# Gated cross-attention and mixture block: the preparation of the next batches laid out anew over the heads, its PSUM banks alternating by batch

## What is computed

```
q = layernorm(x) @ wq + bq ; k = ctx @ wk + bk ; v = ctx @ wv + bv      # 16 heads of width 16
logits = q k^T / sqrt(16) + (1 - mask) * -1e9
attn = softmax(logits) * group_prob
x = x + tanh(g_xattn) * (attn @ v @ wo + bo)
x = x + tanh(g_ffn) * (shared MLP + top-2 of 8 expert MLPs)(rmsnorm(layernorm(x)))
```

## Time and profile before

| | |
|---|---|
| median of 3 runs | 700.69 us |
| the profiled execution | 701.35 us, its span 699.1 us |
| PE busy | 601.9 us (86%) |
| DVE busy | 484.6 us (69%) |
| ACT busy | 394.0 us (56%) |
| POOL busy | 287.0 us (41%) |
| attention's 16 steps | from about 47 us to 344 us of the span |
| granted TensorE clock in the attention | 1.00, 2.4 GHz |
| HBM traffic | 55.43 MB read, 28.30 MB written |

### The profile page before, as it was taken

How to read it: one execution, slowest core, us unless ns; L and a number is a source line. 1 busy time by engine, 2 the same in 40 slices (tenths; PEclk the granted TensorE clock), 3 DMA queues, 4 the chain that set the end, 5 groups by cost and what they waited for, 6 DMA issues and landing times. The chain is left out here.

```text
span 699.1 us, 19138 instructions
## 1 busy us (share of the span) xinstructions
PE 601.9 (86%) x6150; PEld 500.8 (72%) x6150; DVE 484.6 (69%) x1304; ACT 394.0 (56%) x994; POOL 287.0 (41%) x327
## 2 busy tenths in 40 slices
PE   2689999999999999999757999989979989899950
PEld 2457777787777778777536888778868878688850
DVE  5858778877877877778695866565654746556537
ACT  4468888888888888887716423253533434324320
POOL 7303344443443334446530077405535534456120
PEclk9799999999999999999975999999999999899995
DMA  8525557775555655633050042213343332441218
GB/s 226 148 79 145 154 135 190 193 187 131 133 133 137 138 141 138 154 87 68 1 181 1 8 153 99 90 42 128 103 154 119 91 120 91 112 145 46 61 49 311
DMA packets 86600, 84.28 MB, mean 121 GB/s; under 512 B 17879, under 2 KB 80341, under 8 KB 86430
## 3 DMA queue, kind: packets, MB, share of 16 engines
q1 hardware_dynamic: 78686, 70.83, 37.5%
q0 software_dynamic: 2976, 8.16, 3.2%
q10 hardware_dynamic: 4896, 4.76, 2.7%
HBM read 55.43 MB, written 28.30 MB: 120 GB/s over the span
## 5 line engine op out<-in xcount | busy, mean ns | idle before, releaser
L928 PE MATMUL ps<-ident,probs 112*125 112x112 f32 x768 | 192.5, 277 | 2.5 <-POOL probs L509 1.4
L714 ACT ACTIVATE probs<-probs,negmax 112x375 f32<-112x375 f32 x256 | 154.9, 608 | 25.9 <-DVE negmax L1230 25.7
L1082 PE MATMUL ps<-w,arena 128*128 128x256 f16 x1152 | 142.1, 280 | 17.7 <-DVE arena L1373 17.3
L764 ACT ACTIVATE arena<-ps,b 128x256 f32<-128x256 f32 x192 | 79.4, 472 | 137.3 <-PE ps L1071 137.1
L928 PEld LDWEIGHTS ps<-ident,probs 112*125 112x125 f32 x768 | 138.8, 188 | 23.7 <-issue 9.0
L1230 DVE CUSTOM_DVE_ANT_0 probs<-ps,neg 112x375 f32<-112x375 f32 x256 | 137.2, 538 | 11.9 <-issue 9.5
L1082 PEld LDWEIGHTS ps<-w,arena 128*128 128x128 f16 x1152 | 111.4, 100 | 43.7 <-DVE arena L1373 29.0
L509 POOL TENSOR_TENSOR probs<-probs,gp_in 112x375 f32<-112x375 f32 x64 | 58.7, 917 | 181.4 <-ACT probs L714 181.4
L1237 DVE TENSOR_TENSOR arena<-ps,gpT 125x336 f32<-125x336 f32 x192 | 97.0, 506 | 46.4 <-PE ps L928 45.8
L1071 PE MATMUL ps<-probs,w 128*128 128x256 f16 x816 | 91.9, 273 | 0.1
L1071 PEld LDWEIGHTS ps<-probs,w 128*128 128x128 f16 x816 | 79.7, 98 | 9.6 <-issue 0.3
(11 more groups left out here) (173 smaller groups left out, 828.9 us busy)
## 6 DMA issues: line engine op xcount, KB each, us to landing
k_scratch<-kT SPq DMA_DIRECT2D x96, 93.8 KB
kst<-k_scratch SPq DMA_DIRECT2D x64, 140.6 KB, 3.6
w1s<-in_L_ffn_ew_dram SPq DMA_DIRECT2D x8, 1024.0 KB, 5.2
w2s<-in_L_ffn_ew_dram SPq DMA_DIRECT2D x8, 1024.0 KB, 5.6
x_sent<-y_sb SPq DMA_DIRECT2D x12, 516.0 KB, 5.5
ctx_in<-in_ctx_dram SPq DMA_DIRECT2D x16, 375.0 KB
probs<-x_sent ACTq DMA_DIRECT2D x18, 258.0 KB
arena<-y_back SPq DMA_DIRECT2D x7, 512.0 KB, 7.2
```

What stands on the lines that cost most here:

```text
L714: act.activation(probs[:, n % PROBS], probs[:, n % PROBS], ACT.Exp, bias=negmax[:, p, n:n + 1], scale=-1.0, accum_out=rowsum[:, p, ORDER[n ...
L764: act.activation(hid32[:, f], ps[:, f // 2 % 4, f % 2 * TILE:(f % 2 + 1) * TILE], ACT.Relu, bias=b1[:, f, e:e + 1]).then_inc(h_relu, 1)
L928: mm = pe.transpose(ps[0:KP, PT[n % 2], c * S:(c + 1) * S], probs[:, n % PROBS, c * KP:(c + 1) * KP], ident[0:S, 0:S])
L1082: mm = pe.matmul(ps[:, 4 + a, 0:D], hid[:, u, f, a * P:(a + 1) * P], w2[:, p, w, f], start=(f == 0 and j == 0), stop=(f == NF - 1 and j == 2))
```

## The change

The same matmuls are issued; their order, their readers and their banks differ.

- The slots move. Of the batch after next, the context is now at heads 10 and 11 (slots 12 and 13 of the old offset stood at heads 12 and 13) and the keys at heads 12 to 15 (before: head 15 and heads 0 to 2 of the next step). Of the next batch, the values are at heads 2 to 7 (before 5 to 10), chunk 2 first, and the group probability at head 8 (before 11). Heads 0, 1 and 9 have no slot (before 3, 4 and 14). `PREP` is gone.
- `prep_bank(p, piece)` alternates the two banks by piece and by the batch's parity.
- The group probability is taken out of PSUM by DVE (`take_group_probs`, new semaphore `gp_turned`) and no longer by ACT. ACT's pieces stand after its exponentials 0, 1, 5, 9 (keys, keys, values, values), 12 and 13 (context of the batch after next).
- `POOL_HEADS` is (1, 5, 9, 13), was (2, 6, 8, 12). POOL's side work is in another order: `make_neg` after its third head of the step, was after its first.
- DVE makes the keys' low halves at heads 0 and 1 (was 1 and 3), the inverse at 1 (was 0), the division at 13 (was 8).
- SP stores and stacks half 0, then half 1, and loads the mask between storing and stacking half 0. The two stores of high halves no longer wait for the low half.

```diff
-PREP = 4
-        POOL_HEADS = (2, 6, 8, 12)
+        POOL_HEADS = (1, 5, 9, 13)
+        def prep_bank(p, piece):
+            return PR[(p + piece) % 2]
...
                 for n, c in enumerate(K_PARTS):
+                    if c == LO:
+                        sp.wait_ge(in_x[0], 16)
+                        sp.wait_ge(prep_lo, low)
...
                 load_queries(t + 1, 1 - p)
-                for m in range(ND):
-                    store_keys(t + 1, m)
+                store_keys(t + 1, 0)
                 if more:
                     next_mask(t + 1, 1 - p)
-                for m in range(ND):
-                    stack_keys(t + 1, 1 - p, m)
+                stack_keys(t + 1, 1 - p, 0)
+                store_keys(t + 1, 1)
+                stack_keys(t + 1, 1 - p, 1)
...
                     times_group_prob(t, n, p, own if k == 0 else None)
+                    if k == 0 and more:
+                        context_high(t + 2, p, own + 1, turned, slice(0, KC))
                     if k == 0 and not first:
                         spread_inverse(t - 1)
-                    if k == 0 and not last:
+                    if k == 1 and more:
+                        context_low(t + 2, p)
+                    if k == 2 and not last:
                         done = pool.compute_val(H * t + SC_FREE)
                         pool.wait_ge(consts, 4)
                         pool.wait_ge(sc_read, done)
                         make_neg(t + 1, 1 - p, ahead)
-                    if k == 1 and more:
-                        context_high(t + 2, p, own + 1, turned, slice(0, KC))
-                    if k == 2 and more:
-                        context_low(t + 2, p)
...
-            pieces = {0: 1, 3: 2, 5: 3, 11: 4, 13: 5, 14: 6}
+            pieces, context_pieces = {0: 2, 1: 3, 5: 4, 9: 5}, {12: 0, 13: 1}
...
-                    if t_after and n == H - 1:
-                        prep_piece(t + 2, 0, p)
+                    if t_after and n in context_pieces:
+                        prep_piece(t + 2, context_pieces[n], p)
...
+            def take_group_probs(b, p):
+                dve.wait_ge(prep_mm, 7 * b + 7)
+                dve.tensor_copy(gpT[:, p], bank(prep_bank(p, 6), KP, KC * S).rearrange("p (c q) -> p c q", c=KC)).then_inc(gp_turned, 1)
...
-                    if prep and n in (1, 3):
-                        keys_low(t + 1, n // 3)
-                    if n == 0 and not first:
+                    if prep and n in (0, 1):
+                        keys_low(t + 1, n, 1 - p)
+                    if prep and n == 9:
+                        take_group_probs(t + 1, 1 - p)
+                    if n == 1 and not first:
                         invert_sums(t - 1, 1 - p)
-                    if n == 8 and not first:
+                    if n == 13 and not first:
                         divide(t - 1, 1 - p)
```

More of the change, by code:

```diff
@@ L832, in queries, with turn_ctx @@
                     mm.then_inc(q_mm, 1)
-            def turn_ctx(b, k, third):
+            def turn_ctx(b, k, p, third):
                 if third == 0:
@@ L856, in keys @@
                 w, a = PASSES[third]
-                mm = pe.matmul(bank(PR[m], P, S2), wpair[:, 1, w, part, m * P:(m + 1) * P], ctxT[:, a, part, 0:S2],
+                mm = pe.matmul(bank(prep_bank(p, 2 + m), P, S2), wpair[:, 1, w, part, m * P:(m + 1) * P], ctxT[:, a, part, 0:S2],
                                start=(part == 0 and third == 0), stop=(part == 1 and third == 2))
@@ L952, in _ @@
             turn_x(Q_TILES[0])
-            for n in range(2):
+            for n in range(CTX_SLOT, K_SLOT):
                 prep_whole(0, n, 0, 1)
             queries(0)
-            for n in range(2, 7):
+            for n in range(K_SLOT, H):
                 prep_whole(0, n, 0, 1)
             turn_x(Q_TILES[1])
-            for n in range(7, H - 1):
+            for n in range(V_SLOT, GP_SLOT):
                 prep_whole(0, n, 0, 1)
@@ L982, in prep_third @@
                 def prep_third(n, third):
-                    if n + PREP < H and t_next:
-                        prep_slot(t + 1, n + PREP, 1 - p, loads, third)
-                    if n + PREP >= H and t_after:
-                        prep_slot(t + 2, n + PREP - H, p, None, third)
+                    if n < CTX_SLOT:
+                        if t_next:
+                            prep_slot(t + 1, n, 1 - p, loads, third)
+                    elif t_after:
+                        prep_slot(t + 2, n, p, None, third)
                 for n in range(H):
                     turn_probs(t, n, 0)
-                    if first and n == 0:
-                        for m in range(2, PREP):
-                            prep_whole(t + 1, m, 1 - p, loads)
                     prep_third(n, 0)
@@ L1002, in step @@
                     prep_third(n, 2)
+                    if first and n < ND:
+                        for m in range(2):
+                            prep_whole(t + 1, K_SLOT + 2 * n + m, 1 - p, None)
                     if n % QUAD == 1:
@@ L1211, in _ @@
                 queries_low(c)
+            take_group_probs(0, 0)
             dve.wait_ge(small_out, 4)
@@ L1233, in weigh @@
             def weigh(t, n, p):
+                if n == 0:
+                    dve.wait_ge(gp_turned, t + 1)
                 dve.wait_ge(pt_made, 16 * t + n + 1 + PROBS_FREE)
```

78 lines of the change are left out of this document (40 added, 38 removed).

## The result

The change made the kernel slower by 2.75%: the median of five runs is 718.39 us (715.88 to 728.05), that of the kernel before beside it 698.46 us (696.97 to 701.76), the ratio 1.0275 with a 95% interval of 1.0246 to 1.0304. The prediction said 699.6 us, no measurable change, in a range of 688 to 709. It missed in both.

The account below looks back on a forecast made before the run. PE was taken to set the step, so only its idle time could be won. Removed waits (-20.5 us) and new ones (+12.6, +6.8) summed to -1.1 us, from 700.69 to 699.6 us, range 688 to 709.

Parts of the forecast that it names:

- The two waits that go: PE's waits at the value slot (15 x 0.65 us) and second context slot (14 x 0.77) vanish: 20.5 us, bounds 16.3 and 21.4.
- The prediction's first part: What bounds the kernel: PE sets the step, only its idle time can be won, about 1.2 us a step.
- POOL at heads 5 and 13: PE waits for POOL's late products: 0.72 to 0.86 us at head 13, about 0.45 at head 5 (6.8 us in all).
- The stacked keys at head 12, in the loop: PE's score waits 0.8 us for keys stacked behind the mask; with head 13, 0.9 us together, 12.6 us in all.
- the two prices weighed there: Landing of SP's second key stacking: 3.5 or 4.2 us by the trace's rows, 2.3 by the Trainium skill's rule.
- The sum: Whole kernel: -20.5 us for removed waits, +12.6 for heads 12 and 13, +6.8 for head 5, giving -1.1 us.
- The third rival: Second key stacking lands late, PE's score at head 12 waits 1.8 us in 13 steps: 711 us, or 705; chance 0.17.

Follow-up runs that it names:

- The best version: Changed kernel with both stores first, mask last, batch 1's keys before step 0, POOL heads 0, 4, 8, 12, DVE's inverse at head 0, division at 11: ratio 0.9805.
- the variant without a wait for stacked keys: Changed kernel with SP's order as both key stores, both stackings, then the mask's load: ratio 1.0075 against the kernel before.

## Why the prediction was wrong

**The two waits that go: right, but 0.25 us a step too dear.** Both went. I priced them nearer to the weight loads, 0.65 + 0.77 = 1.42 us, and took the matmuls' side (16.3 us for all) for the lower bound. The matmuls' side was the price. In the kernel before a step of 18.80 us has 17.63 of busy PE, so its idle time is 1.17 us. The best version removes nearly all of it and gains 1.1 us a step. The prediction's first part had said "about 1.2 us a step by its matmuls", and its sum then took off more idle time than there was. The term is 16 us and not 20.5.

**POOL at heads 5 and 13: right, head 5 somewhat dear.** Forecast 0.72 to 0.86 us at head 13 and 0.45 at head 5. In the variant without a wait for stacked keys PE idles 0.65 or 0.75 us at head 13 and 0.23 or 0.37 at head 5, by turns. A step with the longer two:

```profile
228.66 0.36 PE L938 MATMUL ps<-ident,probs 112*125 112x112 f32 x1 [0.37 <-POOL probs L514]
...
238.23 0.36 PE L938 MATMUL ps<-ident,probs 112*125 112x112 f32 x1 [0.75 <-POOL probs L514]
```

In the changed kernel itself the wait at head 12 covers that of head 13, as said, and head 5 shows the same 0.23 or 0.37, 0.30 in the mean.

**The stacked keys at head 12, in the loop: right mechanism, somewhat small.** Forecast 0.8, by the landings of the earlier trace rows 1.1 or 1.8; it was 1.17. With 0.30 at head 5 that is 1.47 us of new idle time a step for 1.17 of old, and steps of 19.1 for 18.8. Of the two prices weighed there, that of the rows was the better one: the two stackings of 86.08 took 3.0 and 3.5 us to land, those of half 0 in the loop (229.4) 3.1 and 3.4. The 2.3 us that I had worked out from the Trainium skill ("DMA: Bandwidth & Descriptors") was too short, as the prediction had supposed; the page fits it to DMAs that GpSimd issues, and these are SyncE's. The experiment with `make_neg` at the first head shows the cause to be the one named: the wait goes, and the step is 18.7.

**The first steps: the step that failed, 13.3 us.** The sum had nothing for them. (Of the 13.3 us, 1.5 are the 0.3 us a step of the term above.) The third rival named the mechanism ("the two halves are now stored one after the other, with a landing waited out for each", and the query stores) and then turned it down with the sentence "after them SP still has about 2.5 us to spare in a step". None of the prediction's rows shows that figure, but it was fair for the old order: between the last load and the next store of keys SP stood still for 1.7 to 4.2 us in a round (85.6 to 89.83 in the one above). It was never set against what the new order adds to a round. That is 5.6 us from the first store to the end of the stacking (13.8 against 8.2), more than there was: each half's landing is waited out with nothing to issue but the mask, where before it ran under the other half's stores. A round of 18.8 us less 1.7 to 4.2 and with 5.6 more is 20.2 to 22.7 us, and 20.1 to 22.1 was measured. The rival's price was wrong too. I gave it 0.8 to 1.8 us in each of 13 steps; it was 0.5 to 1.3 us in ten of them and a stall of 3.2 to 3.4 us in three, by turns with the short ones. I read this as a queue that falls behind and is given its time back by PE's long wait. SP's own idle time ahead of the mask fits: 2.0, 1.6 and 1.7 us in the rounds that end in a long wait of PE, 4.0, 4.3 and 6.5 us in those behind them. No run tests that reading. By the orders tried, this part is removed by issuing both stores first, in the changed kernel, and brought in by the new order alone, in the kernel before.

**The clock.** PE's clock was not in the prediction. The table before it gives 1.00 for the whole attention, and that is so from step 1 on, but step 0 had 0.93 already in the kernel before. Of the 5.3 us of the longest step 2.7 are matmuls at half clock. No variant kept a long stall and the clock both, so the split rests on busy times.

**Step 0: not costed, 6.7 us.** The sum counted heads 0 and 1 only for DVE's low keys, in the later steps. In step 0 the keys of batch 1 are made on the spot, in the same two heads as their reader and a POOL head. Moved ahead of the step, they give back 6.0 of it, half of that by the clock. What is left of the difference, 1.1 us, comes with more work: PE has 237 matmuls up to the first inverse there, and 202 in the kernel before, and the last three steps are shorter for it.

**What the range missed.** Its upper end of 709 lay between the third rival's two prices, 705 and 711 us, for a wait of at most 1.8 us in every step. The two terms left out came to 20.0 us at the last inverse, nearly all of the 21.5 that was lost. The other 5.5 us of the two profiled spans lie behind the attention and are not a loss that I can show: the median of the runs is only 19.9 us later.

**Open.** What lets the clock fall in one step and not in another is not shown: a stall of 1.66 us in the kernel before with the new order was followed by the lower clock, one of 1.64 us in the changed kernel with the mask's rows earlier was not. Why the kernel before lost most of its low-key wait with POOL's heads moved was not followed up, nor whether the kernel before would gain from an earlier copy of the group probability alone.

## What to carry to other kernels

Idle time that can be won is the length of the step less the busy time of the engine that sets it; waits in a list for its weight loads and its matmuls are the same time seen twice, and the smaller is the price. A queue that is issued in order is costed by its round, in every stretch of the program with another content (here the steps with query stores, and those with weight loads), and a landing waited out in the middle of it is added to that round and set against what it has to spare. A new layout can be right and show nothing: look for what stands just ahead of the few operations that have a second engine behind them, here an exponential behind a copy and a product behind a split that waits, and move these before judging the layout.

## What the runs showed of the hardware

A stall of PE of 3.38 us in a stretch at 2.4 GHz was followed by 1.2 GHz for the whole of the next window of 4 us, in which 35 matmuls kept PE busy for 4.00 us. Waits of 1.17 us, once in each step of 19.1, left the clock at 1.00. But the length of a wait does not tell by itself: in the kernel before with the new order one of 1.66 us (at 144.17) was followed by 0.57 over the next 4 us, and in the variant with the mask's rows at POOL's first head one of 1.64 us (at 144.65) by 1.00.

The two loads of queries took 1.38 us of SP's queue in step 1 and 5.26 us shortly behind the load of a 1 MB MLP weight, with three smaller DMAs between:

```profile
77.09 1.38 SPq L337 DMA_DIRECT2D arena<-q_scratch  x2
...
134.47 0.44 SPq L394 DMA_DIRECT2D w1s<-in_L_ffn_sw_dram  x1
...
136.91 5.26 SPq L337 DMA_DIRECT2D arena<-q_scratch  x2
```

In the kernel before it is the same: 1.39 us at 84.20, and 3.85 and 4.05 us behind the two weights.
